# Layer kernel on one core: split queries and keys read back in two repeating transfers instead of six

## The reference, cut to what matters

```
h   = modulate(ln(x), shift, scale)
qkv = h @ w_qkv + b_qkv                     # (2, 512, 432)
scores = einsum('bhnd,bhmd->bhnm', q, k) / 3
attn = softmax(scores); out = einsum('bhnm,bhmd->bhnd', attn, v)
```

## Time and profile before

| | us |
|---|---|
| median of 3 runs | 432.49 (430.04 to 434.68) |
| profiled execution, device time | 433.51 |
| its span | 431.6 |

### The profile page before, as it was taken

How to read it: one execution, slowest core, us unless ns; L and a number is a source line. 1 busy time by engine, 2 the same in 40 slices (tenths; PEclk the granted TensorE clock), 3 DMA queues, 4 the chain that set the end, 5 groups by cost and what they waited for, 6 DMA issues and landing times.

```text
span 431.6 us, 6005 instructions
## 1 busy us (share of the span) xinstructions
PE 382.7 (89%) x1986; PEld 168.0 (39%) x1986; DVE 298.2 (69%) x838; ACT 216.1 (50%) x428; POOL 82.8 (19%) x137
## 2 busy tenths in 40 slices
PE   0996679999999988999999888888979999988996
PEld 0333242323324232585856525523323334222555
DVE  7756589898987843463496347798967887942633
ACT  1245007787767774606063220257666776785320
POOL 6897899400101000000000000000001011000000
PEclk9999689999999998999999989969998999999899
DMA  6055543569000000000000441000234000000001
GB/s 183 15 95 150 155 152 89 159 212 253 29 2 3 1 2 0 0 2 1 2 0 2 135 147 50 0 0 2 74 106 143 11 2 2 1 2 0 0 2 55
DMA packets 19657, 24.12 MB, mean 56 GB/s; under 512 B 5404, under 2 KB 15904, under 8 KB 19304
## 3 DMA queue, kind: packets, MB, share of 16 engines
q1 hardware_dynamic: 14360, 21.37, 16.5%
q0 software_dynamic: 3808, 1.73, 2.3%
q10 hardware_dynamic: 1460, 0.66, 0.5%
HBM read 19.38 MB, written 4.14 MB: 54 GB/s over the span
## 4 chain that ended last, share of the span: by engine, by line
PE 67%; DVE 16%; DMA 7%; ACT 4%; SPq 3%; issue 3%; DVEq 0%; ACTq 0%
PE bank L1140 12%; PE bank L1284 10%; DVE nmax L950 9%; PE bank L1244 9%; PE bank L1260 9%; PE bank L1296 9%; PE bank L1270 3%; PE bank L1187 3%; ACT prob L1090 2%; PE bank L1314 2%; DMA Qs<-qk_parts 2%; PE bank L1247 2%; DMA w<-in_L_cond_b_adaln_dram 2%; SPq L480 2%; DMA qk_parts<-prob 1%
## 5 line engine op out<-in xcount | busy, mean ns | idle before, releaser
L950 DVE TENSOR_REDUCE nmax<-bank 128x1 f32<-128x512 f32 x256 | 165.2, 683 | 31.6 <-PE bank L1284 30.9
L1090 ACT ACTIVATE prob<-bank 128x512 f32<-128x512 f32 x256 | 134.8, 603 | 43.2 <-PE bank L1296 42.5
L1284 PE MATMUL bank<-Ks,Qs 81*128 81x512 bf16 x256 | 97.8, 396 | 20.3 <-DMA Qs<-qk_parts 11.4
L1296 PE MATMUL bank<-Qs,Ks 83*128 83x512 bf16 x256 | 96.2, 388 | 5.6 <-ACT prob L1090 4.2
L1140 PE MATMUL bank<-prob,Va 128*32 128x512 f32 x512 | 70.7, 625 | 0.2
L588 POOL DMA_DIRECT2D Qs<-mT x24 | 13.6, 566 | 286.2 <-ACT mT L1097 241.3
L1284 PEld LDWEIGHTS bank<-Ks,Qs 81*128 81x128 bf16 x256 | 25.2, 99 | 87.8 <-DVE nmax L950 46.1
L1079 ACT ACTIVATE big<-bank 128x512 f32<-128x512 f32 (+1 forms) x46 | 27.0, 597 | 47.4 <-PE bank L1247 47.4
L1260 PE MATMUL bank<-w,big 128*128 128x144 f32 (+1 forms) x320 | 44.5, 303 | 0.4 <-DVE nmax L950 0.4
L1260 PEld LDWEIGHTS bank<-w,big 128*128 128x128 f32 (+1 forms) x320 | 37.9, 189 | 6.0 <-DVE nmax L950 1.0
L1296 PEld LDWEIGHTS bank<-Qs,Ks 83*128 83x128 bf16 x256 | 24.9, 99 | 36.3 <-ACT prob L1090 15.7
(11 more groups left out here) (161 smaller groups left out, 411.7 us busy)
## 6 DMA issues: line engine op xcount, KB each, us to landing
Ks<-qk_parts SPq DMA_DIRECT2D x36, 108.0 KB
Qs<-qk_parts SPq DMA_DIRECT2D x36, 108.0 KB
qk_parts<-prob SPq DMA_DIRECT2D x4, 384.0 KB, 2.9
mod<-modulation SPq DMA_DIRECT2D x5, 288.0 KB, 5.2
Ks<-qk_parts SPq DMA_DIRECT2D x6, 216.0 KB
Qs<-qk_parts SPq DMA_DIRECT2D x6, 216.0 KB
w<-in_L_cond_w_dram SPq DMA_DIRECT2D x3, 432.0 KB, 5.3
w<-in_L_cond_w_dram SPq DMA_DIRECT2D x4, 288.0 KB, 3.3
```

The source lines that it names most:

```text
L950: V.tensor_reduce(nmax[:, half, odd * NT + k:odd * NT + k + 1], bank[:, :], AX.X, ALU.max, negate=True).then_inc(s_free, 1)
L1090: A.activation(probs[:, k % 2, j, :], bank[:, :], ACT.Exp, scale=SCALE).then_inc(t_free, 1)
L1284: M.matmul(bank[:, :], Qs[b][0:MROW, h_, k4 * P:(k4 + 1) * P], Ks[b][0:MROW, h_, :], start=True, stop=True).then_inc(s_full, 1)
L1296: M.matmul(bank[:, :], Ks[b][0:SROWS, h0 + k4, k * P:(k + 1) * P], Qs[b][0:SROWS, h0 + k4, :], start=True, stop=True).then_inc(t_full, 1)
```

## The change

The keys are written to DRAM in another order: (column, part, head, token) instead of (part, column, head, token), so that 27 consecutive rows of DRAM are in the order of 27 consecutive rows of `Ks`. For this the transfer of the 128-row key chunk becomes three, one for each part; that of the 16-row chunk stays one. So `qk_out[n]` counts 6 writes instead of 4 (`WRITES`). Reading back, the keys of a piece come in one transfer of 81 rows whose source is 27 rows repeated three times (repeat outermost), and the queries in one transfer of 81 rows whose source is 27 rows, each repeated three times in place (repeat in the middle).

```diff
+WRITES = 6
...
-                        sp.dma_start(parts[w, :, lo:lo + rows, :].rearrange("i r n -> r i n"),
-                                     qkp[n][r:r + rows, c, :, :]).then_inc(qk_out[n], 16)
+                        if w == 0:
+                            sp.dma_start(parts[0, :, lo:lo + rows, :].rearrange("i r n -> r i n"),
+                                         qkp[n][r:r + rows, c, :, :]).then_inc(qk_out[n], 16)
+                            continue
+                        keys = parts[1].rearrange("a r n -> (a r n)").rearrange("(d i m) -> i d m", i=PARTS, d=HD)
+                        keys = keys[:, lo // NH:(lo + rows) // NH, :]
+                        if rows == NH:
+                            sp.dma_start(keys[:, 0, :].rearrange("i (h n) -> h i n", h=NH),
+                                         qkp[n][r:r + rows, c, :, :]).then_inc(qk_out[n], 16)
+                            continue
+                        for i_ in range(PARTS):
+                            sp.dma_start(keys[i_], qkp[n][r:r + rows, c, i_, :]).then_inc(qk_out[n], 16)
...
-                    sp.wait_ge(qk_out[n], 4 * 16)
+                    sp.wait_ge(qk_out[n], 16 * WRITES)
...
-                    src = parts[1].rearrange("j (d h) n -> d j (h n)", h=NH)[:, :, cols]
-                    for i_ in range(PARTS):
-                        r = HD * PARTS * i_
-                        sp.dma_start(Ks[b][r:r + HD * PARTS, lo:hi, :], src).then_inc(done, 16)
+                    src = qk_dram[n, 1].rearrange("a r n -> (a r n)").rearrange("(r m) -> r m", m=NH * N)[:, cols]
+                    src = src.unsqueeze(0).to_broadcast([PARTS, HD * PARTS, (hi - lo) * N])
+                    sp.dma_start(Ks[b][0:PAIRS, lo:hi, :], src).then_inc(done, 16)
                     src = parts[0].rearrange("i (d h) n -> (i d) (h n)", h=NH)[:, cols]
-                    for j in range(PARTS):
-                        sp.dma_start(Qs[b][j:PAIRS:PARTS, lo:hi, :], src).then_inc(done, 16)
+                    src = src.unsqueeze(1).to_broadcast([PARTS * HD, PARTS, (hi - lo) * N])
+                    sp.dma_start(Qs[b][0:PAIRS, lo:hi, :], src).then_inc(done, 16)
...
-                                pe.wait_ge(qk_in[n][piece], 16 * 2 * PARTS)
+                                pe.wait_ge(qk_in[n][piece], 16 * 2)
```

More of the change, by code:

```diff
@@ L1039, in _ @@
                     if n > 1 and first == 0:
-                        act.wait_ge(qk_out[n - 1], 4 * 16)
+                        act.wait_ge(qk_out[n - 1], 16 * WRITES)
                     if n == B:
@@ L1072, in _ @@
                     if stage[:2] == ("mlp1", 0) and lo == 0:
-                        act.wait_ge(qk_out[B * L - 1], 4 * 16)
+                        act.wait_ge(qk_out[B * L - 1], 16 * WRITES)
                     if kind == "fc1" and stage[1:] == (0, 0, 0, CHH):
@@ L1084, in _ @@
                     if g == 0 and k == 0:
-                        act.wait_ge(qk_out[n0], 4 * 16)
+                        act.wait_ge(qk_out[n0], 16 * WRITES)
                     for j in range(G):
```

## The result

The changed kernel is slower: 456.69 us median of 4 runs (452.82 to 460.23) beside 431.26 (4 runs) for the kernel before; the ratio is 1.051, 95% interval 1.044 to 1.058. Its profiled execution took 459.66 us with a span of 457.8, 26.2 more than the 431.6 before. The ratio rests on the two executions at the higher granted clock, 453.72 us (0.94) and 452.82 us (0.947), and leaves out the profiled one (0.933) and 460.23 us (0.932). The forecast was 441.9, 9.4 us more than before, with a range up to 455. It was right in its sign and in its places, but too small: the ratio stands for 22 us, the two profiled executions differ by 26.

A forecast was written before the change was run, and what follows sets the result against it. TensorE bounds most of the chain, with DMA waits at few places: first pieces and two-row maxima transfers. The terms 1.9 + 2.0 + 0.2 + 2.1 + 2.3 + 0.9 = 9.4 us give 441.9 us; range 429 to 455.

The forecast's parts named there:

- Engine counts: DMA engines per transfer, from the outermost count: key read 3, query read 9, write of one key part 8.
- A: Rival: key read spreads over nine engines, first piece lands about 5.8 us after the writes; -2.4 us, 430.1; chance 0.25.
- 2.45 fixed + bytes at 25.6: Landing time of a transfer: 2.45 us fixed, plus its bytes per engine at 25.6 GB/s.
- B: Rival: three engines, but the two-row maxima transfers do not queue behind them; +5.1 us, 437.6; chance 0.15.
- C: Rival: three engines at the lower rate, or SP blocked by a full queue; +16 to +26 us, 449 to 459; chance 0.15.
- Step 2, the writes: Key writes on 8 engines plus two more issues land later: 1.1 us at n = 0 and 2, 0 at n = 3.
- The sign named for it: In the changed profile, a DMA share near 8/16 while the key parts are written.
- Step 3, first pieces: First piece lands 8.2 us after the writes: +0.8, +1.2 and +0.9 us at n = 0, 2 and 3.
- Worth nothing by itself: Reads' issues drop from 84 to 28, freeing SP 3 us sooner per piece; no gain where the engines are late.
- Step 4, pair 0: At n = 0 this pair's two-row maxima transfer queues behind the reads, landing at 69.0, needed at 67.0: +2.0 us.
- Steps 5 and 6, pairs 3 and 5: Layer 0: these pairs' two-row maxima transfers queue behind pieces and late loads: +0.2 and +2.1 us.
- Step 7, POOL's maxima: At n = 1 to 3 otherwise, maxima transfers issued by POOL have a queue of their own: 0 us.

The follow-up runs named there:

- experiment 5: Changed kernel, but at n = 0 and 2 SP issues the second piece only when the first has landed: 458.60 us, ratio 1.060 to the kernel before.
- experiment 1: Changed kernel with the key read's repeat in the middle instead of outermost (key rows land in another order): 435.27 us, ratio 1.007 to the kernel before.
- experiment 9: Changed kernel with the key repeat in the middle, and the second piece of n = 0 and 2 waiting for the first: 432.63 us, ratio 1.003.
- experiment 4: Changed kernel with the eight two-row maxima transfers of n = 0 issued by ACT instead of SP: 453.49 us, ratio 1.048 to the kernel before.
- experiment 2: Changed kernel's six writes in the new DRAM order, read back by six 27-row transfers as before: 431.60 us, ratio 0.999 to the kernel before.
- experiment 6: Kernel before with queries in one 81-row read, and the second piece of n = 0 and 2 waiting for the first: 435.83 us, ratio 1.006.
- experiment 11: Changed kernel with unread filler matmuls in TensorE's waits before n = 0 and slots (1,0) and (2,0): 459.66 us, ratio 1.064 to the kernel before.
- experiment 12: Changed kernel, but first pieces' keys come in three 27-row transfers; only later pieces keep the repeat-outermost key read: 448.87 us, ratio 1.045.

## Why the prediction was right in sign and wrong in size

**Engine counts** held. Three, nine and their place: the share of 0.19 behind pair 5 and in experiment 5, the 19 us that experiment 1 gives back by one exchange, and the share of 0.53 to 0.55, again nine of 16, in the first microseconds of the pieces of experiment 9. The Trainium skill's rule ("DMA: Bandwidth & Descriptors", "Rules for kernel authors": a leading zero-stride broadcast confines a transfer to at most as many engines as it has copies) agrees with this trace. Its way out is to put a dimension outermost whose size is a multiple of 16; experiment 1 puts the 27 rows there and gets nine.

**Rivals.** A fell twice. The key read did not get nine engines, and where it gets them (experiment 9) a piece takes 6.6 to 6.8 us at n = 0 and 2, not 5.8, and nothing is gained (1.003, 0.999 to 1.007). The term "2.45 fixed + bytes at 25.6" is too low where nine engines work together. B fell: pairs 3 and 5 are on the chain. C, three engines at 19.6 GB/s or SP blocked, has the right size (449 to 459, against 456.7). Its arithmetic was near the truth. Of its two causes the rate is borne out; SP was blocked too, 14.58 us, but with the maxima taken off SP the waits at pairs 3 and 5 stay (experiment 4), and only the landing of pair 0 moves.

**Step 2, the writes** (+1.1): confirmed. They land 0.95 us later at n = 0 in experiment 2; counted from the kernel's first matmul they land at 27.4 to 28.3 us in the five traces with the old writes and at 28.3 to 29.6 in the ten with the new ones, 1.1 later in the mean. The sign named for it, a share near 8/16, can't be read alone, since POOL's loads run beside. Not foreseen was that the new order makes a key issue cheap, 0.32 instead of 0.74 us; in the changed kernel this has nothing to act on, as its 81-row key issue takes 0.72.

**Step 3, first pieces**, is the step that failed most: 8.2 us forecast; 10.97, 9.6 and 10.1 measured, 11.6 us on the path instead of 5.1. Two reasons. The rate: 25.6 GB/s holds for three engines alone (experiment 5: 26), but queries and later pieces run on nine at the same time, and there it is 17.4 (experiment 5), and 100 / (0.51 x 16) = 12 at n = 3. I had both ends, 19.6 and 25.6, and chose by the fewest engines; nine were busy. With only its own bytes before it (experiment 5) the first piece still takes 9.52 and 9.10 us, so 1.3 and 0.9 us above the 8.2 are the rate's: 147,456 B less the fixed 2.45 us make 21 and 22 GB/s. The second: I let the first piece see only its own bytes. Issued at once, later pieces delay it: holding the second back gives 1.45 us back here, 1.9 in experiment 6. "Worth nothing by itself" for faster issues was wrong in the other direction: they let the pieces meet.

**Step 4, pair 0** (+2.0): the sum fits (2.1), and so does the mechanism. No wait shows at slot (0,0) in the changed kernel, but by the semaphore events pair 0 lands at 71.04 and the first weight load of the slot starts at 71.10. The wait hides behind TensorE's slow work before it, at a granted clock of 0.52 from 66 to 72:

```profile
66.00:72.00 6.00, 6.00 (x24) 3.00 (x22) 3.54 (x6) 0.03 (x1) 5.49 (x7) 0.52 0.39 109
```

Where TensorE is quicker there, it stands: 2.0 us at full clock in experiment 11, 5.9 and 1.8 us in experiments 5 and 12, each until pair 0 has landed. What the step did not see is that SP's hold puts off the issue itself, to 65.67; it had the transfer issued in time and waiting at the engines.

**Steps 5 and 6, pairs 3 and 5** (+0.2, +2.1): the waits are there, the sizes are 2.6 and 4.9. The queue reckoned at 25.6 GB/s was too short; at 19.6 the forecast had already +5.8 for pair 5. The cause, the engines' load, is what experiments 4 and 12 show.

**Step 7, POOL's maxima** (0): not quite. At 352.78 a two-row transfer issued by POOL took 4.58 us to land, 1.7 before, and the weight load stood 1.00 us for it. An own queue does not protect on shared engines.

**Missing altogether**: the clock. Each longer wait of TensorE was priced at its length alone. The changed kernel has 61 us at half clock, 30 more than before. Experiment 11 shows 4.3 us of the loss to be this; part of the 1.4 behind n = 3 (first matmul 0.61 us, before 0.39) looks alike and is not shown by an experiment. Half clock costs nothing while TensorE stands still, as from 42 to 50 us, so 30 us more of it are not 15 us of loss.

## What to carry to other kernels

Before merging transfers, look which dimension of the source comes outermost and how many engines it leaves: two transfers on three engines lost 5%, the same two on nine lost 0.7%, and with the second piece held back nothing was lost or gained. An issue saved only helps if the engines were waiting for it, and it lets the next transfer run beside the urgent one; count engines first, then issues. And price a wait of TensorE with the half clock that follows it.

## What the runs showed of the hardware that was not expected

- The cost of an issue on SP follows the form of the access, not the rows alone: 27 rows with one stride in DRAM 0.32 us, the same 27 rows with two strides 0.74 us, 81 rows with a repeat 0.7 to 0.8 us. One stride in DRAM is not enough: the query reads of before have it, but go into every third row, and take 0.69 us.
- Behind the reads of n = 0 an issue blocks SP: 4.84, 5.03 and 4.62 us for writes that take 0.57 to 1.24 us where no reads are ahead. That a queue is full then is the likely reason and not shown.
- An engine's rate within one piece ran from 12 GB/s (share 0.51, 100 GB/s) to 209 / (0.58 x 16) = 22.5 GB/s, with 26 when three worked alone. Why it dips to 12 at n = 3 (341 to 343 us), with TensorE, ACT and DVE nearly still, stays open.
- A transfer of 4 KB issued in a queue of its own took up to 8.17 us when other queues had loaded its engines.
